# Linear attention, then gated linear attention with a router: attention part two tiles ahead, transposes by DMA, gated output on GpSimd

## The chip, the cores and the metric

One core of one Trainium2 chip. The metric is the time of one execution on the device, in microseconds, from the first to the last instruction of the core. The engines are TensorE (PE in the rows), VectorE (DVE), ScalarE (ACT), GpSimd (POOL) and SyncE (SP, here only a queue that issues transfers).

## What is computed

Input x is 2 sequences of 4096 rows of 512. Both layers are wrapped as x = x + layernorm(layer(layernorm(x))).

```
# layer 1: linear attention, 16 heads of 32
q, k, v = split(x @ w_qkv.T);  q, k = relu(q), relu(k)
z = 1 / (sum_n k . q + eps);   out = (v k^T) q * z;   out @ w_proj.T + b_proj
# layer 2: gated linear attention, 8 heads of 64, chunks, 1 dense path and 4 experts
q1, k1, v = x @ Wq * s, x @ Wk, x @ Wv
q2 = x @ Wqa @ Wqb * s;  k2 = softmax(x @ Wka @ Wkb)     # per head
gk1, gk2 = log_sigmoid(x @ Wg?a @ Wg?b + bg?) / 16
e = softmax(x @ We);  mask = one_hot(top1(e))            # 4 experts
S_t = diag(exp(gk_t)) S_(t-1) + k_t^T v_t;  o_t = q_t S_t
o = path(q1, k1, gk1) + sum over experts of path(q2*e*mask, k2*e*mask, gk2*mask)
o = rmsnorm(o) * norm_w * silu(x @ Wga @ Wgb);  o @ Wo
```

## The kernel before

The rows are cut into 64 tiles of 128. A first pass makes, for each tile, the normed input, the keys and queries (the queries go out to HBM), and sums up the moments. A short middle part turns the moments into one 512 x 512 matrix (`mix`) for each sequence, so that layer 1 of a tile is a denominator (`den`), a scaling (`ahead_qz`) and one wide product (`y_mm`). The second pass does the rest, tile by tile.

Wide products are done with operands split into a high and a low fp16 part, three matmuls for each (`mm3`); the products of layer 2's recurrence are fp32. Every engine has a program of its own, written out by hand: a function `step(n, ...)` in each lists what that engine does in step n, in order, and the engines meet only in semaphores (`S("name")`). The helpers `cur(n)` and `prev(n)` give the counts that stand for "of tile n" and "of the tile before". An engine that waits holds up everything behind the wait in its own list.

In step n the functions called `front_*` work on tile n, those called `back_*` on tile n-1 (masked scores, carry, selection of the expert's output, join) or on tile n-2 (output product, final norm, store), and those called `ahead_*` on tile n+1 (layer 1: denominator, scaling, product y, residual x1, norm, split into `xn`). TensorE's order in a step is: low-rank product, router product, v, gates, label broadcast, `inter` (sparse and dense product with the state), `intra` (within the chunk), k2, k, `den` of the next tile, q1, transposes of the gated output (`og_transpose`), q2, cumulation, output product (`out_mm`), half sums, y of the next tile, fp32 transposes of q and k, state products, scores of the dense path, transposes of the next tile's normed input (`xn_transpose`), scores of the sparse path.

Both transposes of fp16 data go through PSUM bank 7: eight matmuls against the identity, and then ScalarE copies the bank to SBUF (`ahead_full` to `xnT`, `back_og` to `ogT`). `xnT`, `ogT`, `xn`, `qz` are single buffers; `xb`, `qb`, `x1`, `sil`, `v`, `xr`, `ob` have one slot for even and one for odd tiles (p). The gated output is made by VectorE: `back_normed`, `back_gated`, and `back_split`, which makes the two fp16 parts `og16`. GpSimd sums the masked scores (`back_am`), multiplies v by the experts' masks, scales k2 and makes the state.

SP issues the loads and the stores. In the first pass it also issues one DMA transpose for each tile, of the same size as those that the change adds.

Of the kernel before, what the change touches and what calls it, by code (L numbers as in the profile page):

```python
# [5 lines left out]
P = 128  # L6
KT = C // P
# [39 lines left out]
def sandwich_kernel(nc, x_d, wqkv_d, wproj_d, bproj_d, wb_d, wl_d, ws_d, wo_d, nw_d, consts_d, out_d):  # L47
# [11 lines left out]
    with ExitStack() as ctx:  # L59
# [105 lines left out]
        xmean, wsum = sb("xmean", 2, 1), sb("wsum", KT)  # L165
# [16 lines left out]
        def S(name):  # L182
            if name not in sems:
# [7 lines left out]
                       "xnT_ok", "low1_ok", "labi_ok", "lexp_ok", "abs_ok", "ex_ok", "ln_ok", "sig_ok",  # L191
                       "v_ok", "ke_ok", "e1_ok", "e2_ok", "exs_ok", "q1T_ok", "k1T_ok", "q2T_ok", "k2T_ok",
                       "osq_ok", "ogT_ok", "z_ok", "xc_ok", "xnh_ok", "x1m_ok"],
            "vector": ["xn8_ok", "xf_ok", "kl_ok", "low_ok", "x1_ok", "xn_ok", "am1_ok", "am2_ok", "carry1_ok", "carry_ok", "ldiff_ok",
                       "same_ok", "osum_ok", "ls_ok", "lsl_ok", "sil_ok", "kd_ok", "k1g_ok", "q1g_ok", "q2g_ok",
                       "qz_ok", "on_ok", "og_ok", "out_ok", "hm_ok"],
            "tensor": ["q_pe", "k_pe", "moment_pe", "y_pe", "tr_pe", "a_pe", "t_pe", "u_pe", "low_pe",
                       "ix_pe", "inter_pe", "rx_pe", "route_pe", "g_pe", "o_pe", "k2_pe", "q1_pe", "q2_pe", "cum1_pe", "cum_pe", "sum_pe",
                       "den_pe", "og_pe", "wo_pe", "v_pe"],
            "gpsimd": ["kacc_ok", "am_ok", "vm_ok", "kr_ok", "k2g_ok", "state_ok"],  # L200
# [25 lines left out]
        def _(sp):  # L226
# [7 lines left out]

            def store(j, p):
                wait_alone(sp, S("out_ok"), cur(j * 2 + p))
                sp.dma_start(out_p[bass.ds(j, 1), p, :, :].rearrange("a p c -> (a p) c"), ob[:, p, :]).then_inc(S(f"out{p}"), 16)
# [4 lines left out]
            for name in ("q4_out", "out0", "out1"):  # L242
                sp.sem_inc(S(name), 1)
# [23 lines left out]
            wait_alone(sp, S("q4_out"), 16 * GT * ALL_GROUPS + 1)  # L267
            for p in range(2):
                load(0, p)
            for p in range(2):  # L270
                wait_alone(sp, S("x1_ok"), 2 + p)
                wait_alone(sp, S("qz_ok"), 2 + p)
                load(1, p)
            with sp.Fori(2, ALL // 2) as j:
                for p in range(2):
                    wait_alone(sp, S("x1_ok"), j * 2 + p)
                    wait_alone(sp, S("qz_ok"), j * 2 + p)
                    load(j, p)
                    store(j - 2, p)
            for p in range(2):  # L280
                store(ALL // 2 - 2, p)
# [5 lines left out]
        def _(pe):  # L287
# [11 lines left out]
            def den(n, p, b, ahead=True, back=True):  # L299
                pe.wait_ge(S(f"qb{p}_in"), loads(n, p))  # L300
                if back:
                    pe.wait_ge(S("sel_ok"), (n - 2) * 4 + 4)
                if ahead:
                    pe.wait_ge(S("carry_ok"), n)
                for g in range(KT):
                    last = mm(bank[0][:, g * P:(g + 1) * P], kden[:, b, g, :], qb[:, p, g, :], start=True, stop=True)  # L306
                last.then_inc(S("den_pe"), 1)

            def y_mm(n, b):
                pe.wait_ge(S("qz_ok"), cur(n))  # L310
                mm(bank[0], ones16[:, :], bias16[:, :], start=True, stop=False)
                for g in range(KT):
                    last = mm3(bank[0], lambda x: qz16[:, x, g, :], lambda x: mix[b][:, x, g, :], False, g == KT - 1)
                last.then_inc(S("y_pe"), 1)

            def xn_transpose(n, again):
                pe.wait_ge(S("xn_ok"), cur(n))
                if again:
                    pe.wait_ge(S("osum_ok"), n)
                    pe.wait_ge(S("out_ok"), n - 1)  # L320
                for g in range(KT):
                    for part in range(2):
                        at = (part * KT + g) * P
                        last = nc.tensor.transpose(bank16[7][:, at:at + P], xn[:, part, g * P:(g + 1) * P], ident16[:, :])  # L324
                last.then_inc(S("t_pe"), 1)

            def low_rank(n):
                pe.wait_ge(S("xnT_ok"), cur(n))
# [6 lines left out]
            def route(n):  # L335
                pe.wait_ge(S("am1_ok"), prev(n))
                for g in range(KT):
                    last = mm3(bank[2][:, 0:NEXP], lambda x: xnT[:, x, g, :], lambda x: wl[:, x, g, 2 * P:],
                               g == 0, g == KT - 1)
                last.then_inc(S("route_pe"), 1)  # L340

            def label_bc(n):
                pe.wait_ge(S("labi_ok"), cur(n))
                pe.wait_ge(S("low_ok"), cur(n))
                mm(bank[7][:, 2 * P:3 * P], ones16[:, :], lab_i[:, :], start=True, stop=True).then_inc(S("rx_pe"), 1)
# [87 lines left out]
            def state_products(n, p, ahead):  # L433
# [8 lines left out]
                if ahead:  # L442
                    pe.wait_ge(S("x1_ok"), cur(n + 1))
                for pr in range(PAIRS):
# [8 lines left out]
            def inter(n, front):  # L453
# [14 lines left out]
                last.then_inc(S("ix_pe"), 1)  # L468
                if not front:
                    pe.wait_ge(S("out_ok"), n)  # L470
                if front:
                    pe.wait_ge(S("same_ok"), cur(n + 1))
                for pr in range(PAIRS):
                    last = mm(by_row[:, pr // 2, :, pr % 2, :], q1T[:, pr, :], state0[:, pr, :].rearrange("p (o d) -> p o d", o=2),
                              start=(pr == 0), stop=False, skip_group_check=True)
                last.then_inc(S("inter_pe"), 1)

            def intra(n, p):
                pe.wait_ge(S("am_ok"), cur(n))
                for pr in range(PAIRS):  # L480
                    for odd in range(2):
                        h = 2 * pr + odd
                        last = mm(by_row[:, pr // 2, odd, pr % 2, :], am1[:, odd, pr, :], v[:, p, h * D2:(h + 1) * D2],
                                  start=False, stop=True, skip_group_check=True)
                last.then_inc(S("o_pe"), 1)

            def og_transpose(n, back):
                pe.wait_ge(S("og_ok"), cur(n))
                if back:
                    pe.wait_ge(S("osum_ok"), cur(n + 1))  # L490
                for g in range(KT):
                    for part in range(2):
                        at = (part * KT + g) * P
                        last = nc.tensor.transpose(bank16[7][:, at:at + P], og16[:, part, g * P:(g + 1) * P], ident16[:, :])
                last.then_inc(S("og_pe"), 1)

            def out_mm(n):
                pe.wait_ge(S("ogT_ok"), cur(n))
# [4 lines left out]
            def step(n, p, b, front=True, back=True, tail=True, ahead=True):  # L503
                m, mp, t = n - 1, 1 - p, n - 2
                if front:
                    low_rank(n)
                    route(n)
                    project_v(n)
                    gates(n)
                    label_bc(n)  # L510
                if back:
                    inter(m, front)
# [4 lines left out]
                if ahead:  # L517
                    den(n + 1, mp, b, back=back)
                if front:
                    project_q1(n)  # L520
                if tail:
                    og_transpose(t, back)
                if front:
                    project_q2(n)
                    cumulate(n, back)
                if tail:
                    out_mm(t)
                if front:
                    half_sums(n)
                if ahead:  # L530
                    y_mm(n + 1, b)
                if front:
                    transposes(n)
                    state_products(n, p, ahead)
                    scores(n, 0)
                if ahead:
                    xn_transpose(n + 1, back)
                if front:
                    scores(n, 1)

# [78 lines left out]
            den(0, 0, 0, ahead=False, back=False)  # L619
            context(1)  # L620
            pe.wait_ge(S("mix_ok"), 2)
            y_mm(0, 0)
            mixing(1)
            xn_transpose(0, again=False)
            pe.wait_ge(S("mix_f_ok"), 2 * KT)
            step(0, 0, 0, back=False, tail=False)
# [4 lines left out]
            step(TILES - 2, 0, 0)  # L631
            pe.wait_ge(S("mix1_ok"), 2)
            step(TILES - 1, 1, 1)
            with pe.Fori(TILES, ALL - 2, 2) as n:
                step(n, 0, 1)
                step(n + 1, 1, 1)
            step(ALL - 2, 0, 1)
            step(ALL - 1, 1, 1, ahead=False)
# [5 lines left out]
        def _(act):  # L644
# [21 lines left out]
            def ahead_centre(n, p):  # L666
# [5 lines left out]
            def ahead_norm1(n):  # L672
                act.wait_ge(S("y_pe"), cur(n))
                rstd_of(n, 0, bank[0], eps_y)

            def ahead_norm2(n, p):
# [3 lines left out]
                act.wait_ge(S("t_pe"), prev(n))  # L680
                ac(xn[:, 0], x1[:, p, :], ACT.Copy, scale=rstd[:, 1, :]).then_inc(S("xnh_ok"), 1)  # L681

            def ahead_full(n, p):
                act.wait_ge(S("t_pe"), cur(n))
                act.wait_ge(S("q1_pe"), prev(n))
                ac(xnT.rearrange("p x a b -> p (x a b)"), bank16[7], ACT.Copy).then_inc(S("xnT_ok"), 1)

            def front_residual(n, p, again):
                if again:
                    act.wait_ge(S("out_ok"), n)  # L690
                ac(xr[:, p, :], x1[:, p, :], ACT.Identity, bias=xmean[:, p, :]).then_inc(S("x1m_ok"), 1)

            def ahead_z(n):
                act.wait_ge(S("den_pe"), cur(n))
                ac(bank[0], bank[0], ACT.Ln, bias=eps_z[:, :]).then_inc(S("zln_ok"), 1)
                act.wait_ge(S("zln_ok"), n + 1)
                ac(bank[0], bank[0], ACT.Exp, scale=-1.0).then_inc(S("z_ok"), 1)
# [77 lines left out]
            def back_rms(n):  # L775
                act.wait_ge(S("oms_ok"), n + 2)
                ac(oln[:, :], oms[:, :], ACT.Ln, bias=zero_eps[:, :], scale=1.0 / D2).then_inc(S("oln_ok"), 1)
                act.wait_ge(S("oln_ok"), n + 1)
                ac(ors[:, :], oln[:, :], ACT.Exp, scale=-0.5).then_inc(S("ors_ok"), 1)

            def back_og(n):
                act.wait_ge(S("og_pe"), cur(n))
                act.wait_ge(S("wo_pe"), prev(n))
                ac(ogT[:, :, :, :].rearrange("p x a b -> p (x a b)"), bank16[7], ACT.Copy).then_inc(S("ogT_ok"), 1)
# [5 lines left out]
            def step(n, p, front=True, back=True, tail=True, ahead=True):  # L790
# [740 lines left out]
```

## Time and profile before

| | |
|---|---|
| median of 3 runs | 2654.08 us (2652.09 to 2655.44) |
| the profiled execution | 2656.86 us, its span 2655.1 us |
| TensorE busy over the span | 2538.2 us, 96% |
| VectorE, ScalarE, GpSimd | 1979.1 us (75%), 1629.5 us (61%), 952.8 us (36%) |
| mean granted TensorE clock | 0.994 |

The profiled execution is one of its own, so sums of durations from the trace are to be held against 2656.86, not against the median. The times of the timeline are from the span's start. A timeline row may hold several like instructions (x16); its length runs from the first start to the last end. Matmul records overlap their neighbours, so the distance between starts tells what one costs, not its recorded length. fp32 matmuls leave two records each. What stands in brackets is the idle time of the engine before the row, and who ended it.

### The profile page before, as it was taken

Reading aid. Unit: us, or ns where it says so; the run is one execution under the profiler, and the core shown is the slowest. Engines: PE = TensorE matmul, PEld = TensorE weight load, DVE = VectorE, ACT = ScalarE, POOL = GpSimd, SP = SyncE. Lnnn points to the kernel's source line nnn. Section 1 sums busy time; section 2 is a strip of 40 time slices with the busy share of each in tenths; the row PEclk is TensorE's granted clock in tenths of the full one; section 3 lists DMA queues with packets and bytes.
Section 4 is the critical chain, followed back from the end, with each engine's and each line's share of the span. In section 5 each row is a group of like instructions: output and inputs, shape, how many; then the busy total and the mean of one; then the engine's idle time right before and its main releaser. Section 6 shows DMA issues by size and latency. Waiting matters only on the chain.

```text
span 2655.1 us, 54285 instructions
## 1 busy us (share of the span) xinstructions
PE 2538.2 (96%) x19696; PEld 1579.2 (59%) x19696; DVE 1979.1 (75%) x3740; ACT 1629.5 (61%) x3281; POOL 952.8 (36%) x737
## 2 busy tenths in 40 slices
PE   4999999989999999999999999999999999999997
PEld 2444444456666666666666666666666666666664
DVE  4444444248888888888888888888888888888885
ACT  3222332246777776777777777776777677777774
POOL 2796233223333333333333333333333333333332
PEclk9999999989999999999999999999999999999998
DMA  6434343210000000000000000000000000000000
GB/s 210 115 99 131 98 101 99 56 41 28 24 24 24 24 24 24 24 24 24 24 24 24 27 26 33 24 24 24 24 24 24 24 24 24 24 24 24 24 20 13
DMA packets 115537, 112.12 MB, mean 42 GB/s; under 512 B 72928, under 2 KB 72928, under 8 KB 114976
## 3 DMA queue, kind: packets, MB, share of 16 engines
q1 hardware_dynamic: 104880, 85.75, 11.4%
q10 hardware_dynamic: 9504, 17.31, 1.7%
q0 software_dynamic: 1104, 8.40, 0.9%
q8 instruction: 32, 0.52, 0.1%
q14 instruction: 17, 0.14, 0.0%
HBM read 61.09 MB, written 33.55 MB: 36 GB/s over the span
## 4 chain that ended last, share of the span: by engine, by line
PE 77%; DVE 13%; issue 5%; ACT 2%; POOL 2%; DMA 1%; DVEq 0%; ACTq 0%; SPq 0%; POOLq 0%
PE psum L295 14%; PE psum L297 13%; PE psum L296 13%; PE psum L566 6%; DVE region L1172 6%; PE psum L430 5%; PE psum L466 5%; PE psum L447 4%; PE psum L420 4%; PE psum L306 2%; DVE region L1169 2%; DVE region L1159 2%; PE psum L439 1%; PE psum L350 1%; PE psum L324 1%
## 5 line engine op out<-in xcount | busy, mean ns | idle before, releaser
L295 PE MATMUL psum<-wb,region 128*128 128x512 f16 x768 | 291.8, 380 | 2.4 <-DVE region L1227 2.4
L296 PE MATMUL psum<-wb,region 128*128 128x512 f16 x768 | 291.7, 380 | 0.0
L297 PE MATMUL psum<-wb,region 128*128 128x512 f16 x768 | 291.6, 380 | 0.0
L1013 POOL TENSOR_TENSOR region<-region 128x1024 f32<-128x1024 f32 x64 | 150.2, 2346 | 375.4 <-DVE region L1138 375.4
L1025 POOL TENSOR_TENSOR region<-region,kfac 128x512 f32<-128x512 f32 x64 | 66.8, 1044 | 544.4 <-DVE kfac L1255 544.4
L1008 POOL TENSOR_TENSOR region<-region 128x1024 f32<-128x1024 f32 x64 | 147.9, 2311 | 266.2 <-DVE region L1376 233.6
L1020 POOL TENSOR_SCALAR region<-region,m 128x512 f32<-128x512 f32 x256 | 172.9, 695 | 109.9 <-DVE hm L1208 106.9
L1376 DVE SCALAR_TENSOR_TENSOR region<-psum,region 128x512 f16<-128x512 f32 x64 | 44.3, 692 | 225.3 <-ACT region L841 225.3
L730 ACT ACTIVATE region<-region 128x1024 f16<-128x1024 f32 x64 | 67.6, 1057 | 194.5 <-DVE region L1227 194.5
L566 PE MATMUL psum<-region 128*128 128x512 f16 x768 | 176.2, 379 | 2.2 <-DVE region L1376 2.2
L1124 DVE SCALAR_TENSOR_TENSOR region<-region,rstd 128x512 f16<-128x512 f32 x64 | 48.1, 751 | 140.2 <-ACT region L681 140.2
L1029 POOL TENSOR_TENSOR region<-region 128x512 f32<-128x512 f32 x64 | 81.6, 1276 | 196.7 <-ACT region L752 196.7
L466 PE MATMUL psum<-region 64*128 64x256 f32 x1024 | 129.5, 391 | 22.9 <-DVE region L1159 22.8
L1037 POOL TENSOR_TENSOR region<-region,decay 128x1024 f32<-128x1024 f32 x64 | 150.1, 2345 | 0.0
L1172 DVE SCALAR_TENSOR_TENSOR region<-psum,m,region 128x512 f32<-128x512 f32 x192 | 144.2, 751 | 6.8
L430 PE MATMUL psum<-region 64*128 64x128 f32 x2048 | 148.5, 285 | 0.0
L430 PEld LDWEIGHTS psum<-region 64*128 64x128 f32 x2048 | 124.2, 187 | 31.2 <-issue 24.6
L1372 DVE TENSOR_TENSOR region<-region 128x512 f16<-128x512 f32 x64 | 102.4, 1600 | 49.4 <-ACT region L854 49.4
L664 ACT ACTIVATE region<-psum 128x512 f32<-128x512 f32 x256 | 137.5, 589 | 0.0
L295 PE MATMUL psum<-wqk,region 128*128 128x512 f16 x256 | 97.7, 382 | 34.8 <-DMA region<-region 34.8
L566 PEld LDWEIGHTS psum<-region 128*128 128x128 f16 x768 | 74.9, 98 | 93.6 <-DVE region L1376 3.6
L466 PEld LDWEIGHTS psum<-region 64*128 64x128 f32 x1024 | 105.2, 188 | 42.5 <-issue 42.3
(237 smaller groups left out, 7415.9 us busy)
## 6 DMA issues: line engine op xcount, KB each, us to landing
region<-x_in SPq DMA_DIRECT2D x128, 256.0 KB, 2.6
q_cols<-region ACTq DMA_DIRECT2D x64, 256.0 KB, 2.5
region<-q_cols SPq DMA_DIRECT2D x64, 256.0 KB, 2.8
out_rows<-region SPq DMA_DIRECT2D x62, 256.0 KB, 2.0
region<-wb_in POOLq DMA_DIRECT2D x1, 3072.0 KB, 11.9
region<-wqkv_in SPq DMA_DIRECT2D x4, 512.0 KB, 6.2
region<-ws_in POOLq DMA_DIRECT2D x1, 1280.0 KB, 16.0
mix<-wo_in POOLq DMA_DIRECT2D x1, 1024.0 KB, 18.2
```

The costliest lines, as they stand in the source:

```text
L295: mm(out, lhs(0), rhs(0), start=start, stop=False)
L296: mm(out, lhs(0), rhs(1), start=False, stop=False)
L297: return mm(out, lhs(1), rhs(0), start=False, stop=stop)
L430: last = mm(bank[where[odd]][:, pr * P:(pr + 1) * P], kT[h, pr, :], qT[h, pr, :], start=True, stop=True)
L466: last = mm(psum[:, 2 * half + odd, r * 256:r * 256 + 256], q2T[h, 2 * half + r, :], statex[h, 2 * half + r, :], start=True, stop=True)
L566: last = mm(bank[4 + j], xn8[:, p * GT + t, x * C + j * P:x * C + (j + 1) * P], k16[:, y_, :], start=first and begins, stop=final and ends ...
L664: ac(dst.rearrange("p a b -> p (a b)"), bank[where], ACT.Copy).then_inc(S(done), 1)
L1008: nc.gpsimd.tensor_tensor(kacc[b], kacc[b], k16, ALU.add).then_inc(S("kacc_ok"), 1)
L1013: nc.gpsimd.tensor_tensor(am1[:, :, :, :], am1[:, :, :, :], am2[:, :, :, :], ALU.add).then_inc(S("am_ok"), 1)
L1020: last = nc.gpsimd.tensor_scalar(vm[:, e, :], v[:, p, :], m4[:, p, e:e + 1], 1.0, ALU.mult, ALU.mult)
L1037: nc.gpsimd.tensor_tensor(statex.rearrange("p a (e d) -> p a e d", e=NEXP), carryx.rearrange("p a (e d) -> p a e d", e=NEXP), decay[:, :, ...
L1172: ve.scalar_tensor_tensor(to, of[:, :, e, :], m4[:, p, e:e + 1], to, ALU.mult, ALU.add).then_inc(S("sel_ok"), 1)
```

## The change

The `ahead` functions work on tile n+2 in step n (same slot p as tile n), no longer on n+1; because the slot's mean of the residual would be overwritten, it is kept in `xkeep`. Both fp16 transposes are DMA transposes issued by SP, `turn_xn` (waits for q1 of the tile before and for `xn`) and `turn_og` (waits for the output product before and for `og16`); TensorE's transposes and ScalarE's copies are gone. `back_normed` and `back_gated` move from VectorE to GpSimd, behind the state; the high fp16 part is made by ScalarE at the end of its step (`back_og_high`), the low part by GpSimd at the end of its own (`back_og_low`). Router and low-rank product of tile n+1 stand last in TensorE's step n, and ScalarE's `front_low` for n+1 at the end of its step. The router's logits move from bank 2 to bank 7, the label row from bank 7 to bank 6, and the gates wait for the label masks that read it. The dense state product and the within-chunk product are issued for 64 output rows at a time, two matmuls in place of one. VectorE's list starts with the carry; its label comes before the low parts, its log-sigmoid after the key maximum, its key factor before the low split. The output product stands ahead of the cumulation, q1 behind it.

```
 TensorE, step(n):
-    low_rank(n); route(n); project_v(n); gates(n); label_bc(n); inter(m); intra(m, mp)
-    project_k2(n); project_k(n); den(n + 1); project_q1(n); og_transpose(t); project_q2(n)
-    cumulate(n); out_mm(t); half_sums(n); y_mm(n + 1); transposes(n); state_products(n)
-    scores(n, 0); xn_transpose(n + 1); scores(n, 1)
+    project_v(n); label_bc(n); inter_sparse(m); gates(n); inter_dense(m); intra(m, mp)
+    project_k2(n); project_k(n); den(n + 2); out_mm(t); cumulate(n); project_q1(n)
+    project_q2(n); half_sums(n); y_mm(n + 2); transposes(n); state_products(n)
+    scores(n, 0); scores(n, 1); route(n + 1); low_rank(n + 1)
...
 def gates(n):
     pe.wait_ge(S("low_ok"), cur(n))
     pe.wait_ge(S("am1_ok"), prev(n))
-    pe.wait_ge(S("am2_ok"), prev(n))
+    pe.wait_ge(S("same_ok"), cur(n))
...
 def intra(n, p):
...
-            last = mm(by_row[:, pr // 2, odd, pr % 2, :], am1[:, odd, pr, :], v[:, p, h * D2:(h + 1) * D2],
+            for rows in (slice(0, HALF), slice(HALF, P)):
+                last = mm(by_row[rows, pr // 2, odd, pr % 2, :], am1[:, odd, pr, rows], v[:, p, h * D2:(h + 1) * D2],
...
 SP, loop over j, p (n = 2j + p):
-    reload(j, p); store(j - 2, p)
+    turn_xn(j * 2 + p + 1)
+    store(j - 1, p)
+    reload(j + 2, p)
+    turn_og(j * 2 + p - 1)
...
+def turn_xn(n):
+    wait_alone(sp, S("q1_pe"), prev(n))
+    wait_alone(sp, S("xn_ok"), cur(n))
+    sp.dma_start_transpose(xnT.rearrange("p x a b -> p (x a) b"), xn.rearrange("p x c -> p (x c)")).then_inc(S("xnT_in"), 16)
+def turn_og(n):
+    wait_alone(sp, S("wo_pe"), prev(n))
+    wait_alone(sp, S("og_ok"), cur(n))
+    sp.dma_start_transpose(ogT ..., og16 ...).then_inc(S("ogT_in"), 16)
...
 GpSimd, step(n):
     back_am(n - 1); front_vm(n, p); front_k2(n); front_state(n)
+    back_gated(n - 1, 1 - p)      # og = osum * ors; og = og * sil
+    back_og_low(n - 1)            # og16 low = og - og16 high, waits for ogh_ok
...
 ScalarE, step(n):
-    low(n) label v gates0 router gates1 sig_high square(m) ke sig z(n+1) og_copy(t) exps
-    rms(m) norm3(t) exs centre(n+1) norm1(n+1) transposed norm2(n+1) transposed2 xnT_copy(n+1) residual
+    label v mean centre(n+2) gates0 router gates1 ke square(m) sig_high sig z(n+2) exps
+    rms(m) norm3(t) exs residual norm1(n+2) transposed norm2(n+2) transposed2 low(n+1) og_high(m)
...
 VectorE, step(n):
-    masks(m) carry1 masks2 router low label carry onehot masks select(m) prob logsig join(m) kmax
-    kdiff lslow kfac sil norm(m) qz(n+1) gated_1 gated_q2 normed(m) gated(m) out(t) decay split(m)
-    residual(n+1) ahead_low(n+1)
+    carry1 carry masks(m) masks2 router label low onehot masks select(m) prob join(m) kmax
+    kdiff logsig norm(m) kfac lslow sil qz(n+2) gated_1 gated_q2 out(t) decay
+    residual(n+2) ahead_low(n+2)
```

## Rows read from the trace of the kernel before

**Rows 1.** Busy time of each engine in a window of the second pass.
```profile
core 0: us, PE busy (x) PEld busy (x) DVE busy (x) ACT busy (x) POOL busy (x), PEclk, DMA share, GB/s
1000.00:1320.00 320.00, 311.75 (x2693) 207.40 (x2693) 269.14 (x528) 228.20 (x459) 108.46 (x90) 1.00 0.07 25
```

**Rows 2.** One line's instructions: GpSimd's L1029, durations in ns, first and last start.
```profile
L1029 POOL TENSOR_TENSOR region<-region x64: 1271/1276/1282, 591.6 to 2614.5; 128x512 f32<-128x512 f32 x64
```

**Rows 3.** Timeline of one step, TensorE: start us, length us, group.
```profile
1300.51 1.91 PE L420 MATMUL psum<-cst,region 128*128 128x128 f32 x16
1302.35 0.69 PE L439 MATMUL psum<-region 128*64 128x64 f32 x16
1302.94 1.95 PE L447 MATMUL psum<-region 128*64 128x256 f32 x16
...
1305.91 0.62 PE L324 MATMUL psum<-ident,region 128*128 128x128 f16 x8
...
1311.89 0.59 PE L349 MATMUL psum<-ws,region 128*128 128x512 f16 x2
...
1313.24 2.00 PE L466 MATMUL psum<-region 64*128 64x256 f32 x16 [0.27 <-DVE region L1159]
1315.17 1.16 PE L474 MATMUL psum<-region 128*128 128x128 f32 x8
1316.16 1.90 PE L483 MATMUL psum<-region 128*128 128x64 f32 x16
1318.55 0.39 PE L350 MATMUL psum<-ws,region 128*128 128x512 f16 x1 [0.48 <-DVE region L1172]
...
1325.06 0.61 PE L494 MATMUL psum<-ident,og 128*128 128x128 f16 x8
...
1329.79 0.38 PE L311 MATMUL psum<-bias,ones 128*128 128x512 f16 x1
```

**Rows 4.** One line's instructions: the DMA transposes of the first pass (L246).
```profile
DMA to landing us min/median/max: 3.0/3.0/18.6
```

**Rows 5.** Timeline of the same step, VectorE.
```profile
1304.96 0.75 DVE L1124 SCALAR_TENSOR_TENSOR region<-region,rstd 128x512 f16<-128x512 f32 x1 [2.17 <-ACT region L681]
1306.03 1.29 DVE L1130 TENSOR_TENSOR region<-psum,cst 128x512 f32<-128x512 f32 x2 [0.32 <-PE psum L430]
...
1310.15 0.42 DVE L1185 SCALAR_TENSOR_TENSOR region<-psum,region 64x256 f16<-64x256 f32 x1
...
1313.15 0.17 DVE L1208 TENSOR_TENSOR hm<-m,cst 128x8 f16<-128x8 f32 x1
...
1315.38 0.75 DVE L1169 TENSOR_SCALAR region<-psum,m 128x512 f32<-128x512 f32 x1 [1.52 <-PE psum L466]
...
1318.71 1.76 DVE L1227 SCALAR_TENSOR_TENSOR region<-psum,region 128x1536 f32<-128x1536 f32 x1
...
1322.31 1.22 DVE L1236 SCALAR_TENSOR_TENSOR region<-region 128x1024 f16<-128x1024 f32 x1
...
1332.52 1.42 DVE L1113 TENSOR_TENSOR og<-og 128x512 f16<-128x512 f32 x1
```

**Rows 6.** Timeline of the same step, GpSimd.
```profile
1309.48 2.34 POOL L1013 TENSOR_TENSOR region<-region 128x1024 f32<-128x1024 f32 x1 [5.93 <-DVE region L1138]
...
1324.71 1.04 POOL L1025 TENSOR_TENSOR region<-region,kfac 128x512 f32<-128x512 f32 x1 [8.52 <-DVE kfac L1255]
...
1332.22 1.16 POOL L1036 TENSOR_TENSOR region<-region,decay 128x512 f32<-128x512 f32 x1 [2.10 <-DVE decay L1272]
```

**Rows 7.** One line's instructions: a split on VectorE in the first pass.
```profile
L1372 DVE TENSOR_TENSOR region<-region x64: 693/1768/1773, 15.3 to 495.6; 128x512 f16<-128x512 f32 x64
```

**Rows 8.** Timeline of the same step, ScalarE.
```profile
1309.20 0.38 ACT L704 ACTIVATE region<-psum 64x256 f16<-64x256 f32 x1 [0.99 <-PE psum L297]
...
1311.70 0.40 ACT L711 ACTIVATE lab_i<-ident,lab 128x128 f16<-128x128 f16 x1 [1.58 <-DVE lab L1200]
...
1312.95 1.45 ACT L726 ACTIVATE region<-psum 128x1536 f32<-128x1536 f32 x1 [0.23 <-PE psum L351]
...
1315.99 1.48 ACT L722 ACTIVATE region<-region 128x1536 f32<-128x1536 f32 x1
```

More of the change, by code:

```diff
@@ L441, in state_products @@
                 pe.wait_ge(S("e2_ok"), cur(n))
-                if ahead:
-                    pe.wait_ge(S("x1_ok"), cur(n + 1))
-                for pr in range(PAIRS):
+                for pr in (2, 3, 0, 1):
+                    if pr == 0 and ahead:
+                        pe.wait_ge(S("x1_ok"), cur(n + 2))
                     for odd in range(2):
@@ L501, in out_mm, with step @@
                 last.then_inc(S("wo_pe"), 1)
-            def step(n, p, b, front=True, back=True, tail=True, ahead=True):
+            def step(n, p, b, front=True, back=True, tail=True, ahead=True, more=True, first=False):
                 m, mp, t = n - 1, 1 - p, n - 2
                 if front:
-                    low_rank(n)
-                    route(n)
                     project_v(n)
-                    gates(n)
                     label_bc(n)
                 if back:
-                    inter(m, front)
+                    inter_sparse(m, front)
+                if front:
+                    if first:
+                        pe.wait_ge(S("x1_ok"), cur(1))
+                    gates(n)
+                if back:
+                    inter_dense(m, front)
                     intra(m, mp)
@@ L534, in step @@
                     state_products(n, p, ahead)
+                if front:
                     scores(n, 0)
-                if ahead:
-                    xn_transpose(n + 1, back)
-                if front:
                     scores(n, 1)
+                if front and more:
+                    route(n + 1, tail, back)
+                    low_rank(n + 1)
             def keys(g, p, t):
@@ L623, in _ @@
             mixing(1)
-            xn_transpose(0, again=False)
+            y_mm(1, 0, at=5)
             pe.wait_ge(S("mix_f_ok"), 2 * KT)
-            step(0, 0, 0, back=False, tail=False)
+            route(0, out=False, join=False)
+            low_rank(0)
+            step(0, 0, 0, back=False, tail=False, first=True)
             step(1, 1, 0, tail=False)
@@ L822, in step @@
                 if ahead:
-                    ahead_norm2(n + 1, 1 - p)
+                    ahead_norm2(n + 2, p)
                 if front:
                     front_transposed2(n)
-                if ahead:
-                    ahead_full(n + 1, 1 - p)
-                if front:
-                    front_residual(n, p, tail)
+                if front and more:
+                    front_low(n + 1)
+                if back:
+                    back_og_high(m)
             def norm_tile(u):
@@ L912, in _ @@
                 step(n + 1, 1)
-            step(ALL - 2, 0)
-            step(ALL - 1, 1, ahead=False)
+            step(ALL - 2, 0, ahead=False)
+            step(ALL - 1, 1, ahead=False, more=False)
             step(ALL, 0, front=False, ahead=False)
@@ L1458, in _ @@
                 step(n + 1, 1, 1)
-            step(ALL - 2, 0, 1)
+            step(ALL - 2, 0, 1, ahead=False)
             step(ALL - 1, 1, 1, ahead=False)
```

284 lines of the change are left out of this document (147 added, 137 removed).

## The prediction

> **What bounds the kernel now.** I read the page first (its slices show a first part up to about 560 us and then a very even one), then a window of the even part, one group's first and last start, and one step of the timeline, engine by engine. The change touches nothing of the first pass except what sits behind it in the queues, so all of it is judged in the second. There TensorE is busy 97% at full clock, VectorE 84%, ScalarE 71%, GpSimd 34%, the DMA engines 7% [rows 1]. The first and last start of one GpSimd instruction, 63 steps apart, give the period: (2614.5 - 591.6) / 63 = 32.11 us [rows 2]. A step of TensorE's timeline has only two waits in it, 0.27 and 0.48 us, both for VectorE [rows 3]. So TensorE is the bound, and work taken off it is worth its time, but only until a loop through the other engines is as long. That loop is what has to be found, because the profile of before hides it under 97%.
>
> **What leaves TensorE.** Each step has two batches of eight fp16 transposes, recorded at 0.62 and 0.61 us; a record carries some 0.17 us of pipeline tail (the dense product of the state starts at 1315.17, is recorded at 1.16, and the next group starts at 1316.16), so 0.45 each, 0.9 together. The within-chunk product (L483) is 16 records with 128-column weights in 1.75 us, 0.11 each. It becomes 32 records with 64-column weights, alternating between the two halves of the output rows. The nearest row is L439: 64-column weights, alternating halves, 64 columns moved, 16 records from 1302.35 to 1302.94, 0.037 each. 32 x 0.037 = 1.2, so 0.6 less. The dense state product (L474, 0.99 to the next group) becomes 16 such records with 128 columns; L447 does 256 columns in 1.78 / 16 = 0.11, half of that is 0.055, 16 of them 0.9: 0.1 less. Bounds for both: if the halves do not overlap, 32 records at L483's own pace are 3.5 and 16 are 1.8, 2.6 us worse than now; at L439's pace for both, 0.4 better than I take. I take the value of L439, since it has the same shape, the same alternation and a shared bank. With the two waits gone TensorE would need 32.11 - 0.9 - 0.6 - 0.1 - 0.75 = 29.75 us a step [rows 3].
>
> **The transposes on SP's queue.** The same form of transfer, one tile of 128 x 1024 fp16, lands 3.0 us after issue in the first pass [rows 4]. The one for the input of step n+1 may go when the last product with the old one (q1) is done, which ends q2, half sums and y (0.8 + 2.8 us) before the fp32 transposes, and is needed 7 us after their start: 10.5 us for 3. The gated output's may go at about the start of a step, and its product comes 10 us later. SP's order is: input transpose, store, reload, gated-output transpose; each waits for something later in the step than the one before, so nothing is held. The store and the reloads of tiles two further on have most of a step. Priced at nothing; the cover is those 7 us on either side. ScalarE loses its two PSUM copies of 1024 columns, and gains a conversion of 512 columns (0.6: L726's 1.45 is for 1536) and a tiny copy.
>
> **What GpSimd takes over.** VectorE loses two products of 512 columns, a cast and a split of 1.42 us [rows 5], some 3 us in all. GpSimd gets the two products, 1.04 (the broadcast shape, L1025) and 1.28 (L1029's), and the subtraction, 1.2 like them: 3.5 us [rows 2, 6]. It had 21 us idle, so its load is no matter, but its position is: the products stand directly behind the state update, and the subtraction waits for ScalarE's conversion and stands ahead of the sum of the masked scores.
>
> **Two engines and one door.** The split of the gated output starts at 1332.52, just behind the start of GpSimd's L1036 (1332.22 to 1333.38), and takes 1.42 us; 1333.38 plus 0.56 is its end at 1333.94 [rows 5, 6]. In the first pass, where GpSimd works most of the time, the same shape has a minimum of 693 ns and a median of 1768 [rows 7]. I take it that an instruction that reads PSUM and SBUF has no part in this: the pair of L1130 is 0.65 apiece. So an instruction of VectorE with two SBUF inputs waits for the end of a GpSimd instruction that is under way. The Trainium skill (SBUF — State Buffer, Who interferes with whom) says that for two SBUF inputs the later of the two blocks fully until the other ends; the trace agrees, by the 1.42 us. The Trainium skill (Perfetto Trace Analysis, Optimizing Scalar/DVE Operations) adds that moving work between the two engines might not help for that reason, which speaks against this change; by its rule the sum is the one below, and without any blocking it would be that of the first rival.
>
> **The loop, in the new order.** Zero is the start of the fp32 transposes. ScalarE and VectorE still make tile n+2's residual and its norm here, and VectorE asks for the low part of the normed tile (L1124, two SBUF inputs) at 4.45 (1304.96 - 1300.51) [rows 3, 5]. GpSimd: q1 ends 3.65 before zero, four VectorE instructions of 0.65 (half of L1130) lead to the decay at -1.0, the state runs 1.16 + 2.34 from -0.9, the gated products 1.04 + 1.28 with a hop between: until 5.0. L1124 is caught and ends at 5.6 where it would at 5.2 at latest; bounds 0 and 1.2. Then VectorE has the stretch from L1130 to L1208, the same instructions in another order, 1313.15 - 1306.03 = 7.1 us: it asks for the one-hot halves (L1208: eight elements, but two SBUF inputs) at 12.7. TensorE ends the low-rank product at 8.3 (L349's start less 12 matmuls of 0.216, less zero, less the 0.45 taken out); ScalarE's three copies (as from L704 to L1185, 0.95) and the conversion end at 10.0, GpSimd's subtraction at 11.2, and the sum of the masked scores (L1013, 2.34) at 13.6 [rows 3, 5, 6, 8]. L1208 is caught for 0.9 us. Behind it are the two label masks (0.6), on which the gates now wait, because the label row has moved to their bank: gates at 14.25. The label itself and the sparse product are not later: they leave VectorE 1.9 us earlier (low parts, 1.55 from L1185 to L711's start, and the one-hot masks come behind now), which with L711 and 1.93 of product ends at 13.4. From the gates: 1.06 to ScalarE's L726, 4.52 to the end of L722 (1317.47 - 1312.95), so 19.85; then VectorE's log-sigmoid 1.70, the sum of squares 0.65, the key factor 1.05 and the low split 1.22 (L1236), 24.5, where TensorE's cumulation waits. TensorE then has cumulation, q2 and half sums, 4.73 from L494 to L311 less 0.45 and less the output product of 2.59, so 1.69; q1 2.59; y from L311 to the next zero, 2.83: 31.55 us [rows 3, 5, 8]. The selection chain (L1169 to L350, 3.17, from 14.1) ends at 17.3, as TensorE does with its 3 us of gates, dense and intra, so it adds nothing.
>
> **Sum.** A step goes from 32.11 to 31.55. Some 62 steps: -35 us. Edges: two tiles ahead means a second denominator, norm and residual in the prologue (about +5, ScalarE's and VectorE's part of one tile), the last tile's gated output is 3 us slower by GpSimd and transfer, and one more step at the end runs without its ahead part (-4): +4. The profiled execution lies at 2656.9 (span 2655.1), 2.8 above the median of the runs: 2656.9 - 35 + 4 - 2.8 = 2623 us, 1.2% faster.
>
> **Rivals.** *The door costs nothing or half.* Without either block the gates start at 12.8 and the step is 30.1: 2656.9 - 125 + 4 - 2.8 = 2533; with one of them 30.7 to 31: about 2580. For it: positions decide, and each block needs two starts to meet within a microsecond. Against: both overlaps come out of the order itself. 27%. *TensorE stays the bound*, all chains hidden: 29.75, 2512 us. Against: the walk has slack nowhere. 4%. *Slower: the key factor and the low split.* VectorE now issues the key factor and directly behind it the low split of the log-sigmoids (two SBUF inputs). The factor releases GpSimd's L1025 (1.04). Before, the instruction between them read PSUM. If GpSimd gets in first, the split is 1.04 us later, on the loop: 32.6 a step, 2656.9 + 30 + 4 - 2.8 = 2688. It decides once the loop is 0.56 longer than I have it. For it: nothing but a semaphore hop lies between the two starts. Against: VectorE's own next instruction needs no hop. 20%, with halves that don't overlap (2.6 us of TensorE before k2, partly hidden: 2690 to 2760) in it. *The change doesn't do what it says*, the transfers late: needs 7 us beyond 3.0; 2%. The rest, 5%, are small misses that leave it level.
>
> **Numbers.** The forecast's own case (2600 to 2648) has 42%. A measurement tells 0.2% (5 us) from no change. Faster 0.72, within 0.07, slower 0.21. The range reaches from between the first rival's two values to the slow case, 2545 to 2682; the likeliest case's own range is 2600 to 2648.
>
> **What would show it.** L1124 at about 1.1 instead of 0.75 us; the one-hot product far above 0.17; TensorE waiting for the label, then for the label masks ahead of the gates, then for the low split ahead of the cumulation, some 2 us a step in all, busy about 93%; no wait for a transfer; within-chunk product near 1.2 us. The prediction is wrong if those two VectorE instructions keep their length (then 2533), if the low split is longer than 1.22 (then slower than before), or if 64-column halves don't overlap.

## The result, and the profile after

The changed kernel takes 2659.76 us (median of 12 runs, 2657.15 to 2663.22), the kernel before on the same chip 2653.58 (2651.28 to 2656.12): ratio 1.0023, 95% interval 1.0015 to 1.0032. It is slower by a hair, where 2623 and a gain were forecast. TensorE is busy for 121 us less than before, and the span has not moved. The page after, engines and TensorE's line of the slices:

```profile
PE 2416.8 (91%) x20208; PEld 1433.8 (54%) x20208; DVE 1884.5 (71%) x3484; ACT 1554.8 (59%) x3281; POOL 1191.1 (45%) x929
PE   4999999989999989999999999999999899999997
```

Busy times in the same window as in [rows 1]:

```profile
1000.00:1320.00 320.00, 292.81 (x2740) 184.29 (x2740) 253.91 (x486) 215.40 (x458) 145.09 (x120) 1.00 0.16 41
```

The GpSimd instruction of [rows 2], now L1054:

```profile
L1054 POOL TENSOR_TENSOR region<-region x64: 1262/1271/1275, 590.3 to 2618.8; 128x512 f32<-128x512 f32 x64
```

And the landing of the 64 new transposes of the input and of the 64 of the gated output, as in [rows 4]:

```profile
DMA to landing us min/median/max: 3.0/3.0/4.7
```
```profile
DMA to landing us min/median/max: 3.0/3.0/3.6
```

The step is (2618.8 - 590.3) / 63 = 32.20 us, before 32.11: 63 x 0.09 = 6 us slower in all. What lies around those 63 steps went from 2655.1 - 2022.9 = 632.2 to 2655.4 - 2028.5 = 626.9, 5 us faster. TensorE is busy for 311.75 / 320 of a step before and 292.81 / 320 after: 31.3 and 29.5 us. The 1.8 us have turned into waits. The timeline of one step shows where, TensorE first:

```profile
1300.88 0.38 PE L336 MATMUL psum<-bias,ones 128*128 128x512 f16 x1
1303.68 1.91 PE L437 MATMUL psum<-cst,region 128*128 128x128 f32 x16
...
1314.63 0.22 PE L362 MATMUL psum<-lab_i,ones 128*128 128x128 f16 x1
1314.78 2.00 PE L483 MATMUL psum<-region 64*128 64x256 f32 x16
1318.43 0.59 PE L366 MATMUL psum<-ws,region 128*128 128x512 f16 x2 [1.66 <-DVE same_c L1264]
...
1319.39 1.09 PE L492 MATMUL psum<-region 128*64 128x128 f32 x16
1320.31 1.10 PE L503 MATMUL psum<-region 128*64 128x64 f32 x32
1321.36 0.39 PE L367 MATMUL psum<-ws,region 128*128 128x512 f16 x1
...
1328.83 0.38 PE L418 MATMUL psum<-region,centred 128*128 128x512 f16 x1 [0.79 <-issue]
```

The gates (L366) wait 1.66 us for the label masks and the cumulation (L418) 0.79. The products by halves come out near their forecast: L492 0.92 from start to start, L503 1.05 (forecast 0.9 and 1.2; L474 and L483 in [rows 3] 0.99 and 1.75). VectorE in the same step:

```profile
1305.22 0.75 DVE L1162 SCALAR_TENSOR_TENSOR region<-psum,rstd,region 128x512 f32<-128x512 f32 x1 [2.21 <-issue]
1308.21 0.75 DVE L1166 SCALAR_TENSOR_TENSOR region<-region,rstd 128x512 f16<-128x512 f32 x1 [2.25 <-ACT region L704]
...
1315.35 2.09 DVE L1248 TENSOR_SCALAR m<-cst,lab 128x4 f32<-128x4 f32 x1
1317.48 0.17 DVE L1251 TENSOR_TENSOR hm<-m,cst 128x8 f16<-128x8 f32 x1
1317.68 0.35 DVE L1263 SCALAR_TENSOR_TENSOR same_d<-psum,lab,cst 128x128 f16<-128x128 f32 x1
1317.94 0.34 DVE L1264 SCALAR_TENSOR_TENSOR same_c<-psum,lab,cst 128x128 f32<-128x128 f32 x1
...
1324.05 1.76 DVE L1270 SCALAR_TENSOR_TENSOR region<-psum,region 128x1536 f32<-128x1536 f32 x1 [0.48 <-ACT region L741]
...
1327.40 1.22 DVE L1281 SCALAR_TENSOR_TENSOR region<-region 128x1024 f16<-128x1024 f32 x1
```

and GpSimd:

```profile
1304.10 1.91 POOL L1062 TENSOR_TENSOR region<-region,decay 128x1024 f32<-128x1024 f32 x1
...
1307.08 1.28 POOL L1073 TENSOR_TENSOR og<-og,region 128x512 f32<-128x512 f32 x1
1313.95 1.16 POOL L1078 TENSOR_TENSOR og<-og 128x512 f16<-128x512 f32 x1 [5.59 <-ACT og L804]
1315.07 2.35 POOL L1038 TENSOR_TENSOR region<-region 128x1024 f32<-128x1024 f32 x1
...
1327.58 1.94 POOL L1050 TENSOR_TENSOR region<-region,kfac 128x512 f32<-128x512 f32 x1 [7.08 <-DVE kfac L1300]
```

From ScalarE, its first copy of the low-rank product and the conversion to the high part:

```profile
1312.24 0.38 ACT L723 ACTIVATE region<-psum 64x256 f16<-64x256 f32 x1 [3.09 <-PE psum L321]
...
1313.18 0.63 ACT L804 ACTIVATE og<-og 128x512 f16<-128x512 f32 x1
```

L1248, an instruction on four elements for each row, takes 2.09 us: it starts at 1315.35, 0.28 us behind GpSimd's sum of the masked scores (L1038), and ends at 1317.44, when that ends (1317.42). The label masks are behind it in VectorE's list, and the gates behind those. The other direction is there too: L1050, 1.04 us in [rows 6], takes 1.94, behind VectorE's low split (L1281, two SBUF inputs), which has started 0.18 us ahead of it. L1162, which reads PSUM, runs wholly beside GpSimd's L1062 and keeps its 0.75 us.

### The profile page after: what moved, and what is told of

The parts are those of the page before. It is cut to its first block, busy times and chain, and to the rows that moved or that the text cites. A ratio compares the mean times of both kernels' runs of the same rounds, so it can differ in the third digit from the quotient of the medians.

```text
span 2655.4 us, 56298 instructions
## 1 busy us (share of the span) xinstructions
PE 2416.8 (91%) x20208; PEld 1433.8 (54%) x20208; DVE 1884.5 (71%) x3484; ACT 1554.8 (59%) x3281; POOL 1191.1 (45%) x929
## 4 chain that ended last, share of the span: by engine, by line
PE 59%; DVE 19%; issue 10%; ACT 8%; POOL 2%; DMA 1%; SPq 1%; DVEq 0%; ACTq 0%; POOLq 0%
PE psum L319 12%; PE psum L321 12%; PE psum L320 12%; PE psum L580 6%; DVE m L1248 5%; DVE region L1172 3%; DVE region L1201 2%; PE psum L492 2%; ACT junk L672 2%; DVE region L1180 2%; PE psum L437 2%; PE psum L503 2%; PE psum L331 2%; PE psum L367 2%; ACT region L704 2%
## 5 line engine op out<-in xcount | busy, mean ns | idle before, releaser
L1050 POOL TENSOR_TENSOR region<-region,kfac 128x512 f32<-128x512 f32 x64 | 124.4, 1944 | 452.7 <-DVE kfac L1300 452.7
L1078 POOL TENSOR_TENSOR og<-og 128x512 f16<-128x512 f32 x64 | 74.0, 1157 | 347.8 <-ACT og L804 347.8
L745 ACT ACTIVATE region<-psum 128x1536 f32<-128x1536 f32 x64 | 92.9, 1452 | 155.3 <-PE psum L368 155.3
L1045 POOL TENSOR_SCALAR region<-region,m 128x512 f32<-128x512 f32 x256 | 172.3, 692 | 24.9 <-DVE hm L1251 24.9
L1038 POOL TENSOR_TENSOR region<-region 128x1024 f32<-128x1024 f32 x64 | 150.6, 2353 | 8.5 <-DVE region L1180 8.5
L447 PEld LDWEIGHTS psum<-region 64*128 64x128 f32 x2048 | 125.9, 188 | 51.1 <-issue 51.1
L1166 DVE SCALAR_TENSOR_TENSOR region<-region,rstd 128x512 f16<-128x512 f32 x64 | 48.1, 752 | 143.1 <-ACT region L704 143.1
L1162 DVE SCALAR_TENSOR_TENSOR region<-psum,rstd,region 128x512 f32<-128x512 f32 x64 | 48.1, 751 | 140.9 <-issue 138.1
L1054 POOL TENSOR_TENSOR region<-region 128x512 f32<-128x512 f32 x64 | 81.2, 1269 | 141.5 <-ACT region L771 141.5
L723 ACT ACTIVATE region<-psum 64x256 f16<-64x256 f32 x64 | 24.1, 377 | 195.8 <-PE psum L321 195.8
L1270 DVE SCALAR_TENSOR_TENSOR region<-psum,region 128x1536 f32<-128x1536 f32 x64 | 112.5, 1758 | 31.9 <-ACT region L741 31.9
L1061 POOL TENSOR_TENSOR region<-region,decay 128x512 f32<-128x512 f32 x64 | 67.0, 1047 | 149.3 <-DVE decay L1317 149.3
```

The costliest lines, as they stand in the source:

```text
L447: last = mm(bank[where[odd]][:, pr * P:(pr + 1) * P], kT[h, pr, :], qT[h, pr, :], start=True, stop=True)
L1038: nc.gpsimd.tensor_tensor(am1[:, :, :, :], am1[:, :, :, :], am2[:, :, :, :], ALU.add).then_inc(S("am_ok"), 1)
L1045: last = nc.gpsimd.tensor_scalar(vm[:, e, :], v[:, p, :], m4[:, p, e:e + 1], 1.0, ALU.mult, ALU.mult)
L1050: nc.gpsimd.tensor_tensor(kd.rearrange("p (h d) -> p h d", h=H2), kd.rearrange("p (h d) -> p h d", h=H2), kfac[:, :].unsqueeze(2).to_broad ...
```

## The experiments

In each the step is read off as above, from the first and last start of the key product on GpSimd, 63 steps apart.

**One-hot masks behind the selection.** Does the blocked mask cost what it seems to, or would the wait for the selection swallow it?

```
 VectorE, step(n), from the changed kernel:
-    front_onehot(n, p)
     front_masks(n)
     back_select(m, mp)
+    front_onehot(n, p)
```

> VectorE makes the one-hot masks (m4, hm) behind the selection, no longer ahead of the label masks. Theory 'the door is on the loop': in the changed kernel the one-hot mask of four elements takes 2.09 us because GpSimd's sum of the masked scores is under way, and the gates wait for the label masks behind it. Here it should take about 0.2 us, TensorE's wait ahead of the gates (1.66 us a step) should go to about 0.1, the step from 32.2 to about 30.7, the time to 2565 us (2550 to 2590). Rival 'swallowed': the key product waits for the selection anyway, and the selection starts behind the sparse product, which nothing blocks; then at most 0.5 us a step of the 1.9 comes back, 2630 us or more.

Measured 2563.9 us, ratio to before 0.9653 (0.9636 to 0.9669), step (2525.4 - 591.1) / 63 = 30.70. One entry of VectorE's list, moved behind the two that followed it, is worth 96 us. The mask by itself, all 64 of them:

```profile
L1248 DVE TENSOR_SCALAR m<-cst,lab x64: 219/219/223, 577.6 to 2515.3; 128x4 f32<-128x4 f32 x64
```

The wait ahead of the gates is gone from the timeline, and TensorE waits for the selection instead (0.39 us), then 0.52 ahead of the cumulation.

**GpSimd's subtraction one place later.** The same from the other side: VectorE's list stays.

```
 GpSimd, step(n):
     back_am(n - 1)
     front_vm(n, p)
+    back_og_low(n - 2)
     front_k2(n); front_state(n); back_gated(n - 1, 1 - p)
-    back_og_low(n - 1)
```

> Only GpSimd's list is changed: the low part of the gated output is subtracted one step later, behind the masked values of the next tile, so that the sum of the masked scores starts as soon as both scores are masked, 1.6 us earlier. VectorE's list is that of the changed kernel. Theory 'the door': the sum ends at about the time at which the one-hot mask is asked for, which then waits 0.4 us or less in place of 1.9; step about 30.8, time 2570 us (2550 to 2600). Rival 'VectorE's own order' (the one-hot mask is slow there for another reason than GpSimd): nothing changes, 2655 to 2665. The transposed output lands 7 us later and should still not be waited for.

Measured 2566.67 us, ratio 0.9660 (0.9644 to 0.9676), step 30.73. The mask still meets the end of the sum, but only that:

```profile
L1252 DVE TENSOR_SCALAR m<-cst,lab x64: 230/551/880, 575.9 to 2512.2; 128x4 f32<-128x4 f32 x64
```

Two edits on different engines give 96 and 93 us, and the meeting of the mask with the sum is what they have in common. The transposed output, now requested some 7 us later, was not waited for in the even part. At the very end it is waited for as in the changed kernel, 6.3 us for the last tile, and twice more at the edges of the second pass (9.1 us in all).

**An extra instruction ahead of the sum.**

```
 GpSimd, step(n):
+    pad = pad + pad        # 128 x 512 fp32, a buffer of its own
     back_am(n - 1)
```

> One more instruction on GpSimd in each step, 128 x 512 fp32 on a buffer of its own (about 1.2 us), between the subtraction for the gated output and the sum of the masked scores. Theory 'the door': the one-hot mask is caught 1.2 us longer (3.3 in place of 2.1) and all of it goes on the step: 33.4 us, time about 2735 (2715 to 2745). Rival 'GpSimd has time': it is idle for 17 us of each step and the sum is needed only 2.9 us after its end, so nothing changes: 2655 to 2665.

Measured 2761.76 us (one run), step 33.83: 1.63 more, where I had put 1.2. Its timeline, VectorE and then GpSimd:

```profile
1318.74 0.79 DVE L1255 TENSOR_SCALAR m<-cst,lab 128x4 f32<-128x4 f32 x1
1319.56 2.27 DVE L1258 TENSOR_TENSOR hm<-m,cst 128x8 f16<-128x8 f32 x1
```
```profile
1318.46 1.04 POOL L1083 TENSOR_TENSOR pad<-pad 128x512 f32<-128x512 f32 x1
1319.46 2.35 POOL L1039 TENSOR_TENSOR region<-region 128x1024 f32<-128x1024 f32 x1
```

The mask gets through where one GpSimd instruction ends, and the next instruction of VectorE is caught by the next of GpSimd: 3.06 us for the two, against 2.26. That is 0.8. The other 0.8 is TensorE's. Its wait ahead of the gates is now 2.44 us, and the two products behind them take 1.77 and 1.62 us from start to start in place of 0.92 and 1.05:

```profile
1322.61 0.59 PE L367 MATMUL psum<-ws,region 128*128 128x512 f16 x2 [2.44 <-DVE same_c L1271]
...
1323.71 1.98 PE L493 MATMUL psum<-region 128*64 128x128 f32 x16
1325.48 1.69 PE L504 MATMUL psum<-region 128*64 128x64 f32 x32
1327.10 0.39 PE L368 MATMUL psum<-ws,region 128*128 128x512 f16 x1
```

Windows of two successive halves of a step, first this kernel, with the stretch of the slow products behind it, then the changed one in a like place:

```profile
1200.00:1216.75 16.75, 16.48 (x174) 11.15 (x173) 11.00 (x25) 10.69 (x30) 8.04 (x7) 1.00 0.23 63
1216.75:1233.50 16.75, 14.07 (x106) 8.45 (x103) 14.91 (x25) 10.68 (x16) 7.52 (x7) 0.90 0.08 16
...
1322.60:1327.10 4.50, 4.49 (x52) 3.62 (x53) 3.10 (x6) 3.25 (x5) 2.09 (x4) 0.62 0.00 0
```
```profile
1200.00:1216.00 16.00, 15.73 (x167) 10.54 (x166) 10.32 (x21) 9.96 (x27) 7.02 (x6) 1.00 0.22 66
1216.00:1232.00 16.00, 13.65 (x113) 7.94 (x111) 15.06 (x30) 11.82 (x20) 7.31 (x7) 1.00 0.09 16
```

The granted clock is 0.90 on the mean of that half step and 1.00 in the other half, as in the other five steps up to 1400 (0.89 or 0.90), and 0.62 over the slow products: for most of them TensorE ran at 1.2 GHz, behind a wait of 2.44 us and not behind one of 1.66. So the door's share (the time that the two blocks take) is 0.8, and the rest is put down to what the slow products push back: VectorE's join of the outputs, which needs them, waits 1.47 us for TensorE there. No run varies the wait and the clock apart.

**The same instruction elsewhere.**

```
 GpSimd, step(n):
     front_vm(n, p)
+    pad = pad + pad
     front_k2(n)
```

> The control for the extra instruction on GpSimd: the same instruction in the changed kernel, but behind the masked values, where VectorE runs instructions with a PSUM input. Theory 'it is the place, not the load': no change, step 32.2, 2655 to 2665 us. Rival 'GpSimd is the bound or the load counts': about 1.1 us a step, 2725 us.

Measured 2658.57 us (one run), step 32.21: nothing. This load is free in one place and costs 1.63 us a step in another.

**The extra instruction ahead of the gated products.** In the changed kernel VectorE's L1166 starts at 1308.21 and keeps its 0.75 us, though GpSimd's L1073 ends at 1308.36 by its record: the first block of the forecast did not come about. (The end of such a record blocks nothing: L1248 ends with the sum's record, and its own 0.22 us lie inside it.) Here the block does come about.

```
 GpSimd, step(n):
     front_state(n)
+    pad = pad + pad
     back_gated(n - 1, 1 - p)
```

> The changed kernel with the extra GpSimd instruction (1.04 us) between the state and the gated products. There it moves the second gated product, which in the changed kernel is just over when VectorE asks for the low part of the normed tile (L1166, two SBUF inputs), to where it covers that moment for 1.2 us. If the low part is stopped as forecast, it takes about 1.8 instead of 0.75 us, every instruction behind it starts a microsecond later, and the step goes from 32.2 to 33.0 or so, about 2710 us. If instructions of this form are not stopped by GpSimd, it keeps 0.75 us and the time stays at 2655 to 2665.

```profile
L1173 DVE SCALAR_TENSOR_TENSOR region<-region,rstd x64: 751/1686/1694, 567.7 to 2570.3; 128x512 f16<-128x512 f32 x64
```

The instruction is stopped, by 0.93 us, as I had expected of this form, but the time is 2660.66 us (one run), where I had put 2710, and the step 32.23: it cost nothing. I had the consequence wrong. In this kernel's step the mask comes 0.9 us later and is let go at the same moment:

```profile
1320.73 1.18 DVE L1255 TENSOR_SCALAR m<-cst,lab 128x4 f32<-128x4 f32 x1
```

The end of the block is not set by VectorE. GpSimd's sum starts behind the subtraction, that behind ScalarE's conversion (L804), that behind ScalarE's copies of the low-rank product. Between the low-rank product and the gates the loop runs through ScalarE and GpSimd, and VectorE has time to spare as long as it asks before the sum is over.

**The sum of squares behind the low split.**

```
 VectorE, step(n):
     front_logsig(n)
-    back_norm(m)
     front_kfac(n); front_lslow(n); front_sil(n, p, tail)
+    back_norm(m)
```

> VectorE sums the squares of the output (norm) behind the low split and silu, no longer ahead of the key factor. Theory 'the low split releases the cumulation': low split 0.6 us earlier (ScalarE's high part is ready by then), TensorE's wait ahead of the cumulation (0.79) mostly gone, step 32.2 to 31.6, time 2622 us (2610 to 2640). Rival: the cumulation is released by something else (GpSimd's key product, the label masks, ScalarE): no change, 2655 to 2665.

Measured 2632.14 us, ratio 0.9906 (0.9889 to 0.9922), step 31.77: 0.43 of the 0.6. TensorE's wait ahead of the cumulation falls from 0.79 to 0.32 us and does not vanish, so the theory holds with a smaller size.

**Both reorderings.** The one-hot masks behind the selection and the sum of squares behind the low split, the two edits of VectorE's list shown above.

> Both reorderings of VectorE's list at once: one-hot masks behind the selection, and the sum of squares behind the low split. The step was 30.7 us with the first alone, with 0.5 us of TensorE's waits ahead of the cumulation. Theory 'one loop in two places': the second takes that half microsecond as well, step 30.2 us, 2533 us (2525 to 2550). Rival 'the first already left TensorE as the bound': no more than 5 us below the first alone, 2558 us or more.

Measured 2535.89 us, ratio 0.9548 (0.9532 to 0.9564), step 30.23. The gains add up.

**Products by halves, undone and alone.** First undone in the changed kernel, then alone in the kernel before:

```
-    for rows in (slice(0, HALF), slice(HALF, P)):
-        mm(by_row[rows, ...], am1[:, odd, pr, rows], v[...])
+    mm(by_row[:, ...], am1[:, odd, pr, :], v[...])          # and the dense state product likewise
```

> The changed kernel with the dense state product and the product within the chunk issued for all 128 output rows at once, as before the change. TensorE needs 0.8 us a step more for them (0.99 and 1.75 against 0.92 and 0.95 or so). Theory 'the loop through VectorE is the bound': TensorE reaches the cumulation 0.8 us later, just when the low split has released it, and the key maximum a little later; at most 0.15 us a step, 2655 to 2670 us. Rival 'TensorE's work counts': 0.8 a step, 2705 to 2712 us.

Measured 2665.81 us, ratio to before 1.0039 (1.0024 to 1.0053), step 32.27: 0.07 us more. The work undone is also less than the 0.8 us that I had put. From the gates to k2 (L367) TensorE now takes 1320.51 to 1323.99, 3.48 us, against 2.93 with halves (1318.43 to 1321.36): 0.55 us. In the new order the whole-row dense product takes 0.89 and not 0.99, and the halves start 0.1 us later behind the gates. The wait ahead of the cumulation falls from 0.79 to 0.32 and takes up nearly all of the 0.55.

> The kernel before with one part of the change alone, the two products issued by halves of the output rows. They run between the sparse product and k2, and k2 waits for VectorE's selection, which starts at the end of the sparse product and takes 3.17 us. Theory: the 0.8 us saved turn into a longer wait ahead of k2 (0.48 to 1.3), no change: 2650 to 2657 us. Rival 'before is bound by TensorE at 97% busy': 0.8 us a step, about 2604 us.

Measured 2654.26 us, ratio 0.9994 (0.9984 to 1.0004). The row of its timeline that answers to the last but two of [rows 3] (wait 0.48 there):

```profile
1318.41 0.39 PE L350 MATMUL psum<-ws,region 128*128 128x512 f16 x1 [1.35 <-DVE region L1175]
```

The saved 0.87 us is all in the wait. So in the kernel before too, 97% busy, a part of TensorE's work was free.

The same edit once more, in the kernel with both reorderings:

> Both reorderings of VectorE's list, with the dense state product and the product within the chunk for all 128 output rows at once. The two cost TensorE 0.8 us more; the wait for the selection ahead of k2, 0.39 us in the kernel with both reorderings, takes the first half of it. Theory: what is left of TensorE's work counts once the loop no longer hides it, 0.4 us a step, 2560 us (2550 to 2570) against 2536. Rival 'the halves are never worth anything': 2536 to 2540. Rival 'the whole 0.8 counts': 2585.

Measured 2535.61 us, ratio 0.9554 (0.9538 to 0.9570), against 0.9548 with halves. My forecast of 2560 missed, by its premise of 0.8 us: from the gates to k2 it is 3.49 us in place of 3.39, since the halves save 0.55 here and the selection had held k2 by 0.39. The last tenth is gone by the start of the cumulation (6.61 us behind k2, 6.72 with halves). So whether TensorE's work would count once it exceeds that wait by more is not shown. In no kernel here are the halves worth more than some 0.2%.

**The router product between the scores.**

```
 TensorE, end of step(n), both reorderings kept:
     scores(n, 0)
+    route(n + 1, tail, back)
     scores(n, 1)
-    route(n + 1, tail, back)
     low_rank(n + 1)
```

> Both reorderings of VectorE's list, and TensorE's router product for the next tile moved from behind both scores to between them. The scores of the sparse path wait 0.27 us for ScalarE's copy of the fourth transpose; the router product (0.31 us) needs nothing of it and fills that wait. Theory: 0.2 to 0.27 us a step, 2520 us (2516 to 2530). Rival 'the wait only moves', to the label or the selection: 2533 to 2540.

Measured 2524.79 us, ratio 0.9519 (0.9503 to 0.9535), step 30.10, the fastest version here. The step is 0.13 us shorter than with both reorderings alone, half of the 0.27 us that were filled; the label broadcast waits longer for ScalarE instead.

## Why the prediction was wrong

**What bounds it.** Right that TensorE's work is worth its time only up to a loop through the others, and right in the loop's places: a one-hot instruction stopped ahead of the gates, the label masks, the low split ahead of the cumulation. Too generous to TensorE all the same: the halves alone show that in the kernel before some 0.8 us of its work already lay in the shadow of the selection (3.17 us, [rows 3, 5]), so that edit could bring nothing there either.

**The step that failed is the loop's length at the one-hot mask.** The prediction says: VectorE "asks for the one-hot halves (L1208: eight elements, but two SBUF inputs) at 12.7", "L1208 is caught for 0.9 us", "gates at 14.25". On the same zero (1303.68) the trace has the instruction ahead of it, L1248, caught from 11.67 to 13.76, one-hot halves and label masks still to do behind the block, and the gates at 14.75. The prediction's rule was for two SBUF inputs, and the mask has one SBUF tensor and a pointer scalar, so the rule left it out; it is stopped like the others. Of the half microsecond, 0.24 is the halves that are still to be made behind the block, 0.16 the later end of the sum (13.76, forecast 13.6), and 0.1 the way from the masks to the gates. From there everything runs as forecast, half a microsecond late, but for one hop: L1270 at 20.4 (19.85), end of the low split at 24.9 (24.5), then a hop of 0.2 us that I had not counted, the cumulation at 25.15, and 4.28 to y and 2.80 for it: 32.2 instead of 31.55. 0.65 x 62 is 40 us, and the edges were 9 us better than I had them (-5 for +4): 31 us, which is the miss against the profiled execution (2626 forecast, 2657.15 measured). The medians differ from the profiled executions by a few us, one downward, one upward, which makes 37 of it. The mechanism was right and its size wrong, and since the whole forecast gain was 35 us, the sign went with it. The prediction's own terms add up to 31.58 where it writes 31.55, which changes nothing.

**The first block** ("L1124 is caught and ends at 5.6") did not happen: GpSimd's products end at 4.7 and not at 5.0, and L1166, asked for at 4.5, keeps its length. The run in which it does happen shows that it is worth nothing: VectorE has slack there until the sum on GpSimd is over. So both instructions that were named as the sign ("if those two VectorE instructions keep their length (then 2533)") kept it, and the time was not 2533: the block had fallen on the mask, which the sign did not name.

**The transfers** priced at nothing: right in the even part, 3.0 us to landing and no wait there, also 7 us later; the last tile's is waited for 6.3 us, which lies in the edges. **The halves**: 0.92 for 0.9 us and 1.05 for 1.2 forecast, but 0.55 saved in all for 0.7, and worth nothing. **What leaves TensorE**: 29.5 us of work a step, 29.75 forecast. **The edges**: forecast +4, measured -5; not looked into.

**The rivals.** "The door costs nothing" was priced at 30.1 a step and 2533 us. Taking the block at the mask away brought 1.50 us a step (32.20 to 30.70), where this price held 1.45; it ends at 30.70 and not at 30.1, since it starts from a step 0.65 longer than the one forecast. The 30.23 and 2536 us with both reorderings are near the price by another way. The slow rival, GpSimd's L1025 getting in ahead of the low split, did not occur: VectorE's instruction was first, and GpSimd's waited (1.94 us). Level had 7%. A forecast gain of 0.56 us a step, at the end of a long chain of hops, several of them known to 0.1 or 0.2 us only, should have left more for it.

## What to carry to other kernels

An engine that is 97% busy can still be on a loop of the same length as another; before taking work off it, walk the loop through the engines that it waits for even briefly, in the new order. When work goes to GpSimd, list what VectorE will ask for while it runs: the size of that instruction does not matter, only its place, and whether what is behind it in the list is waited for. The first thing to try is then to move the small instruction behind those that read PSUM: here that was worth 96 us net. And measure what an edit saves in the order in which it will stand: 0.8 us in the order before were 0.55 in the new one.

## What the runs showed of the hardware

A VectorE instruction of four fp32 elements with one SBUF tensor and a pointer scalar waited for the end of a GpSimd instruction, up to 1.9 us (2.09 against 0.22), as those with two SBUF tensors did (1.69 against 0.75, 2.27 against 0.17); a VectorE instruction with a PSUM input beside one did not (L1162, 0.75 us in all 64 steps). Whoever starts first has it: GpSimd's product took 1.94 instead of 1.04 us behind a VectorE split. Between two GpSimd instructions without a gap one VectorE instruction got through (the mask, 0.79 us, in the kernel with the extra instruction). And TensorE's granted clock stayed at 1.00 with a wait of 1.66 us in each step, but fell to 0.90 on the mean of the half step in the kernel with one of 2.44 us, and that kernel lost 1.63 us a step where the blocks explain 0.8.
